# Sums over the values in three rounded fp32r products, and spread over three slots, in a two-layer cross-attention kernel

## Reference

```python
def _cross_attention(q_in, kv_in, wq, bq, wk, bk, wv, bv, wo, bo, bias_k, bias_v):
    qh = (q_in @ wq + bq).reshape(b, q_len, H, K)        # H = 16, K = 128
    kh = (kv_in @ wk + bk).reshape(b, t, H, K)
    vh = (kv_in @ wv + bv).reshape(b, t, H, K)
    kh, vh = (each with one more key, bias_k or bias_v, at the end)
    logits = jnp.einsum('bqhk,bthk->bhqt', qh, kh) / sqrt(K)
    weights = jax.nn.softmax(logits, axis=-1)
    ctx = jnp.einsum('bhqt,bthk->bqhk', weights, vh).reshape(b, q_len, H * K)
    return ctx @ wo + bo

x = x + _cross_attention(layer_norm(x), context, weights 1)
x = x + _cross_attention(layer_norm(x), context, weights 2)
x = x + gelu(layer_norm(x) @ w_fc1 + b_fc1) @ w_fc2 + b_fc2
```

## Time and profile before

| | |
|---|---|
| three timed executions | 1518.45, 1424.64, 1518.13 us; median 1518.13 |
| the profiled execution | 1426.43 us, its span 1424.7 us |
| PE | busy 1366.2 us, 96% of the span, 11607 matmul records |
| DVE, ACT, POOL | busy 902.9 us (63%), 620.4 us (44%), 307.6 us (22%) |

### The profile page before, as it was taken

The page is one execution under the profiler, slowest core; times in us unless marked ns, Lnnn a source line. Parts: engine busy times, 40 slices in busy tenths (PEclk is TensorE's granted clock), DMA queues, the critical chain, the costliest instruction groups (busy, mean ns, idle before and its releaser), DMA issues. The chain is left out here.

```text
span 1424.7 us, 27588 instructions
## 1 busy us (share of the span) xinstructions
PE 1366.2 (96%) x11607; PEld 1219.9 (86%) x11607; DVE 902.9 (63%) x1876; ACT 620.4 (44%) x1022; POOL 307.6 (22%) x290
## 2 busy tenths in 40 slices
PE   5999999999999999999999999998898999997898
PEld 4889998999999898999999999987887877776787
DVE  4866667576666777666666666668534378886322
ACT  4633433434343564334343434346422337775421
POOL 2201011010110112011011010112863023334654
PEclk9999999999999999999999999999999999998999
DMA  5100000001100000000000000000000000002000
GB/s 154 60 31 1 30 11 21 30 1 31 30 2 31 1 31 1 30 31 1 30 1 31 31 2 30 10 22 23 1 1 9 0 2 2 2 3 64 5 30 29
DMA packets 28012, 30.53 MB, mean 21 GB/s; under 512 B 684, under 2 KB 26868, under 8 KB 27892
## 3 DMA queue, kind: packets, MB, share of 16 engines
q1 hardware_dynamic: 27668, 28.72, 6.3%
q10 hardware_dynamic: 226, 0.10, 0.0%
HBM read 26.73 MB, written 2.10 MB: 20 GB/s over the span
## 5 line engine op out<-in xcount | busy, mean ns | idle before, releaser
L334 POOL TENSOR_TENSOR WLO<-W,WHI 128x512 fp32r<-128x512 f32 x64 | 80.7, 1290 | 765.9 <-DVE WHI L728 765.9
L761 DVE STREAM_TRANSPOSE PRT<-PR 32x256 f32<-32x256 f32 x512 | 223.2, 436 | 8.4
L768 DVE TENSOR_TENSOR CLO<-bank,CHI 128x512 fp32r<-128x512 f32 x128 | 88.0, 691 | 145.6 <-ACT CHI L649 145.6
L626 ACT ACTIVATE KT<-bank,PH 128x512 f32<-128x512 f32 x128 | 88.0, 688 | 186.1 <-PE bank L171 186.1
L169 PE MATMUL bank<-WHI,CHI 128*128 128x256 f32 x576 | 167.5, 291 | 0.0
L170 PE MATMUL bank<-WLO,CHI 128*128 128x256 f32 x576 | 161.5, 280 | 0.0
L171 PE MATMUL bank<-WHI,CLO 128*128 128x256 f32 x576 | 161.0, 280 | 0.0
L169 PE MATMUL bank<-WHI,SRC_HI 128*128 128x256 f32 x504 | 146.2, 290 | 0.0
L170 PE MATMUL bank<-WLO,SRC_HI 128*128 128x256 f32 x504 | 140.9, 280 | 0.0
L171 PE MATMUL bank<-WHI,SRC_LO 128*128 128x256 f32 x504 | 140.8, 279 | 0.0
L791 DVE TENSOR_TENSOR X<-X,bank 128x512 f32<-128x512 f32 x128 | 88.0, 688 | 68.0 <-PE bank L171 67.4
(11 more groups left out here) (230 smaller groups left out, 3124.2 us busy)
## 6 DMA issues: line engine op xcount, KB each, us to landing
W<-in_wall SPq DMA_DIRECT2D x17, 1024.0 KB, 5.6
W<-in_ctx SPq DMA_DIRECT2D x4, 512.0 KB, 6.8
X<-in_x SPq DMA_DIRECT2D x4, 512.0 KB, 8.6
mlp_w<-in_w SPq DMA_DIRECT2D x2, 1024.0 KB, 9.1
out<-X SPq DMA_DIRECT2D x4, 512.0 KB, 2.9
W<-in_wall SPq DMA_DIRECT2D x1, 512.0 KB, 6.5
W<-in_wall SPq DMA_DIRECT2D x2, 256.0 KB, 8.3
W<-in_qw SPq DMA_DIRECT2D x1, 256.0 KB, 2.8
```

The costliest lines, as they stand in the source:

```text
L334: i = e.tensor_tensor(WLO[a][:, j, :, :], W[a][:, j, :, :], WHI[a][:, j, :, :].bitcast(F32), ALU.subtract)
L626: e.activation(KT[:, h, :, 0:S], PROJ[2 + h][:, :].rearrange("p (q k) -> p q k", k=S), ACT.Identity, bias=PH[:, 1, 2 * pair + h:2 * pair + ...
L761: i = e.transpose(PRT[b * S + z:b * S + z + 32, :, b * S + y:b * S + y + 32], PR[b * S + y:b * S + y + 32, :, z:z + 32])
L768: e.tensor_tensor(CLO[:, h, :], bank[3 + h][:, :], CHI[:, h, :].bitcast(F32), ALU.subtract).then_inc(c_lo, 1)
```

## The change

The values are now kept as a rounded part `VH` (written by ACT in `values_out`) and a remainder `VLW` (written by DVE in `values_rest`). The transposed softmax weights `PRT` get a rounded part `PHI` (ACT, `probs_hi`) and a remainder `PLO` (POOL, `probs_lo`). `weighted` makes 24 fp32r matmuls of 128 columns through `three()` in place of eight in fp32. PE's order in a slot is now keys, output(n - 2), queries, values 0, values 1, scores(n), weighted(n - 1): a weighted sum follows its scores by one slot and its output by two. The other engines' orders follow, and so does the head of the feed-forward block.

```diff
+            VH = [sb(f"VH{a}", [P, GT, 256], F32R, scope=ph) for a in range(2)]
+            VLW = [sb(f"VLW{a}", [P, GT, 256], F32R, scope=ph) for a in range(2)]
...
@@ gpsimd
+                    def probs_lo(u):
+                        for h in range(2):
+                            e.wait_ge(p_hi, 2 * u + h + 1)
+                            part = slice(h * GT, (h + 1) * GT)
+                            e.tensor_tensor(PLO[:, part, :], PRT[:, part, :], PHI[:, part, :].bitcast(F32),
+                                            ALU.subtract).then_inc(p_lo, 1)
...
+                        before = apply_at(n - 1)
+                        if before is not None:
+                            norm_lo(e, norm, *before)
...
+                        if n:
+                            probs_lo(n - 1)
+                        if g == 2 and pair + 1 < NL * HP + 1:
                             split(pair + 1, 1 - a)
@@ tensor
                     def weighted(u):
-                        e.wait_ge(v_out, 2 * u + 2)
-                        e.wait_ge(pt_out, u + 1)
+                        e.wait_ge(v_lo, 2 * u + 2)
+                        e.wait_ge(p_lo, 2 * u + 2)
                         if u:
                             e.wait_ge(x_settled, 2 * u)
                         for h in range(2):
                             for p in range(GT):
-                                i = e.matmul(bank[3 + h][:, p * P:(p + 1) * P],
-                                             V[u % 2][:, p, h * K:(h + 1) * K],
-                                             PRT[:, h * GT + p, :], start=True, stop=True)
+                                ks = slice(h * K, (h + 1) * K)
+                                i = three(e, bank[3 + h][:, p * P:(p + 1) * P], VH[u % 2][:, p, ks],
+                                          VLW[u % 2][:, p, ks], PHI[:, h * GT + p, :], PLO[:, h * GT + p, :],
+                                          True, True)
                             i.then_inc(c_done, 1)
...
                         keys(n)
...
+                        if n == 2:
+
+                            weighted(0)
+                        elif n > 2:
+                            output(n - 2)
...
                         queries(n)
                         values(n, 0)
...
-                        weighted(n - 1)
                         values(n, 1)
...
                         scores(n)
-                        output(n - 1)
+                        if n > 1:
+                            weighted(n - 1)
...
-                    for q in range(4):
-                        up(q)
+                    up(0)
+                    up(1)
+                    output(SLOTS - 2)
+                    up(2)
+                    up(3)
                     e.wait_ge(sub_done, SLOTS)
                     bias_turns(NL - 1, G - 1, (TB[1], None), SLOTS - 1)
                     weighted(SLOTS - 1)
+                    up(4)
                     e.wait_ge(ptb_out, NL * G)
                     norm_turn(e, norm, NL, 1, TB)
+                    up(5)
                     output(SLOTS - 1)
-                    e.wait_ge(fc2_lo, 1)
+                    up(6)
+                    up(7)
                     e.wait_ge(norm.scaled, (NL * G + 2) * DC)
                     norm_turn(e, norm, NL, 2, TB)
@@ scalar
+                    def probs_hi(u):
+                        e.wait_ge(pt_out, u + 1)
+                        for h in range(2):
+                            part = slice(h * GT, (h + 1) * GT)
+                            e.activation(PHI[:, part, :], PRT[:, part, :], ACT.Copy).then_inc(p_hi, 1)
...
                     for n in range(1, SLOTS):
...
+                        if n > 2:
+                            weighted_out(n - 2)
+                        exponential(n - 1)
...
                         keys_out(n)
...
+                        probs_hi(n - 1)
                         queries_out(n)
                         values_out(n, 0)
...
-                        weighted_out(n - 1)
                         values_out(n, 1)
...
-                        exponential(n)
@@ vector
+                    def values_rest(n, j):
+                        e.wait_ge(v_out, 2 * n + j + 1)
+                        e.tensor_tensor(VLW[n % 2][:, 2 * j:2 * j + 2, :],
+                                        (PROJ[2 + j] if n else PROJ[j])[:, :].rearrange("p (t n) -> p t n", n=256),
+                                        VH[n % 2][:, 2 * j:2 * j + 2, :].bitcast(F32), ALU.subtract).then_inc(v_lo, 1)
...
+                        if n >= 2:
+                            weighted_rest(n - 2)
...
                         softmax(n - 1)
...
+                        if n >= 2:
+                            settle(n - 2)
...
-                        weighted_rest(n - 1)
                         if g == 2 and pair + 1 < NL * HP + 1:
                             round_set(pair + 1, 1 - a)
...
+                        values_rest(n, 0)
+                        values_rest(n, 1)
                         shifted(n)
-                        settle(n - 1)
```

More of the change, by code:

```diff
@@ L345, in _ @@
                                     ALU.subtract).then_inc(w_split, 1)
[L346 to L348 removed]
+                    def probs_lo(u):
[4 more added lines that the diff above has]
+                                            ALU.subtract).then_inc(p_lo, 1)
+                    for n in range(SLOTS):
+                        pair, a, g = unit(n)
+                        before = apply_at(n - 1)
+                        if before is not None:
+                            norm_lo(e, norm, *before)
+                        if apply_at(n) == (NL, 0):
+                            norm_lo(e, norm, NL, 0)
+                        if n:
+                            probs_lo(n - 1)
+                        if g == 2 and pair + 1 < NL * HP + 1:
                             split(pair + 1, 1 - a)
[L350 to L351 removed]
+                    probs_lo(SLOTS - 1)
                     e.wait_ge(fc2_hi, 1)
@@ L363, in _ @@
                         if q == 1:
+                            norm_lo(e, norm, NL, 1)
+                        if q == 3:
+                            norm_lo(e, norm, NL, 2)
                             e.wait_ge(fc2_hi, 2)
@@ L540, in _ @@
                         if bias is not None:
-                            e.wait_ge(q_out, 2 * n + 2)
-                            bias_turns(*bias, PROJ, n - 1)
-                        weighted(n - 1)
[L544 to L550, removed]
+                            if last_turn:
+                                e.wait_ge(norm.scaled, (NL * G + 1) * DC)
+                            else:
+                                e.wait_ge(sub_done, n)
+                            bias_turns(*bias, (TB[1], TB[0]), n - 1)
+                        if n == 2:
+                            output(0)
+                        values(n, 1)
+                        if turned_now is not None and not last_turn:
+                            e.wait_ge(q_out, 2 * n + 2)
                             norm_turn(e, norm, *turned_now, PROJ)
+                        if bias is not None:
+                            L, bg = bias
+                            e.wait_ge(ptb_out, L * G + bg + 1)
+                            e.wait_ge(bw_out, L + 1)
                         if g == 0:
@@ L665, in _ @@
                     queries_out(0)
-                    for c in range(DC):
-                        scale_chunk(e, 0, 1, c, PROJ)
-                    exponential(0)
                     ctx_round(2)
@@ L671, in _ @@
                     for n in range(1, SLOTS):
-                        bias, took, now = bias_at(n), stats_at(n), apply_at(n)
+                        bias, took, before = bias_of(n - 1), stats_at(n), apply_at(n - 1)
+                        if n > 2:
+                            weighted_out(n - 2)
+                        exponential(n - 1)
+                        if before is not None:
+                            for c in range(DC):
+                                scale_chunk(e, *before, c, PROJ)
                         keys_out(n)
@@ L675, in _ @@
                             ctx_round(3)
+                        if n == 2:
+                            weighted_out(0)
+                        if apply_at(n) == (NL, 0):
+                            for c in range(DC):
+                                scale_chunk(e, NL, 0, c, TB)
+                        probs_hi(n - 1)
                         queries_out(n)
@@ L678, in _ @@
                         if bias is not None:
-                            bias_out(*bias, PROJ[0])
-                        weighted_out(n - 1)
+                            bias_out(*bias, TB[1])
                         values_out(n, 1)
-                        if now is not None and now[0] == NL:
-                            for c in range(DC):
-                                scale_chunk(e, *now, c, PROJ)
-                        elif now is not None:
```

(4 more changed lines are left out.)

117 lines of the change are left out of this document (68 added, 49 removed).

## The result

| kernel | median of 4, us | lowest, highest |
| --- | --- | --- |
| before | 1472.61 | 1424.64, 1518.45 |
| after | 1525.63 | 1480.38, 1570.94 |

The ratio is 1.0383 with a 95% interval of 1.0339 to 1.0428: slower, as forecast. Each kernel's four executions are two pairs some 90 us apart (before 1424.6 and 1427.1, then 1518.1 and 1518.5; after 1480.4 and 1480.6, then 1570.6 and 1570.9), and the ratio compares the shorter pairs. The execution of after that was profiled is a longer one, 1570.64 us; those 90 us lie in one stretch behind the slots, so the slots can be read against those of before as they are.

A forecast was written before the change was run, and what follows sets the result against it. The prediction took PE, busy 96% of the span, as the bound. Products +57.3, layer-norm slots +4 and feed-forward head -7 gave +54 us on 1426.4, 1480.8, ratio 1.038; scaled to the median, 1576, range 1465 to 1610.

The forecast's parts named there:

- the load is the floor: Weighted sums on PE: loading 128 stationary columns sets each fp32r product's pace, 0.1115 us; this case has 65%.
- Rival 1: Weighted sums: columns, not the load, set the price, 58 ns or less a product; kernel faster, 1399 us, ratio 0.981; 7%.
- rival 2: Weighted sums: loads partly overlap, a product between 0.074 and 0.1 us; 1434 us, 1526 on the median; 9%.
- rival 3: Weighted sums: short fp32r matmuls fall to fp32's rate, 0.213 us a product; 1636 us, ratio 1.147; 12%.
- The products: Weighted sums on PE: 24 fp32r products, 2.68 us, replace 1.78; +0.90 us a slot, +57.3 us over 64.
- The other engines: Slots: added work on DVE (88 us), POOL (168) and ACT (some 77) never reaches PE; costed at nothing.
- rival 4: Slots: the longer chain over ACT, DVE and POOL starves PE; 1 us each slot gives +64, 1545 us; 7%.
- The slots with the layer norm: About ten slots where DVE's cover is thin: 0.5 us each allowed, +4 us, bounds 0 and 15.
- The head of the feed-forward block: At its start most of PE's 5.7 us wait for POOL goes: -7 us, bounds -12 and +2.
- The sum: Whole kernel: 57.3 + 4 - 7 = +54 us on the profiled 1426.4, giving 1480.8, ratio 1.038.
- The median: Whole kernel: ratio applied to the median, 1518.1 x 1.038 = 1576 us; 1481 if it falls among shorter executions.

The follow-up runs named there:

- experiments 3 and 4: Changed kernel, all slots but the first: 3 with 64 moving columns in weighted sums, 1494.71 to 1495.39 us; 4 with 64 stationary columns, 1405.73, 1407.07, 1496.24, 1496.29.
- experiment 2: Changed kernel with two fp32r products in place of three in each weighted sum, third operand still made: 1425.59, 1426.15, 1516.72 and 1517.1 us.
- experiment 1: Changed kernel with plain fp32 weighted sums, remainders still made and waited for: 1424.59 to 1428.24 us in seven executions, 1516.92 to 1519.35 in three.
- experiment 5: Changed kernel's order with plain fp32 sums, no rounded parts or remainders: 1514.17 to 1517.23 us in six executions, ratio 1.0618 to before.
- experiment 9: Changed kernel's order with fp32 sums, plus ten extra fp32r matmuls ahead of the small-attention loop: median 1424.14 us, ratio 0.9968 to before.

## Why the prediction was right

**The step that decides: the load is the floor.** Forecast 0.1115 us a product, measured 0.111, with half the moving columns 0.111, with half the stationary columns 0.059. Rival 1 (columns) and rival 2 (loads that overlap) fall with experiments 3 and 4, rival 3 (fp32's rate of 0.213) with the slot of 15.18. That an fp32r load keeps the pace of an fp32 one was inferred from durations alone (188 and 193 ns before, 192 after); experiment 2 shows it, 16 records of either kind in a slot of 14.29. The figure of 107 ns from the Trainium skill, "TensorE: Matmul & The Clock Gate", LDWEIGHTS, is 4% under what the products show; its rule that the price goes with the loaded columns agrees with 0.111 and 0.059. The gap of about 81 ns in the same page's Back-to-back issue gap is not what any run here shows for fp32r with 128 loaded columns. (Rival 2 called 0.081 the middle of 0.074 to 0.1; the middle is 0.087, which would have made it +20 us for the slots and not +10.)

**The products.** Forecast +0.90 us a slot and +57.3 in all; measured +0.89 against fp32 sums in the same order (15.18 - 14.29), +0.87 against before, and 54.4 in all. The difference lies in the first slots. The second and third distances between scores are 18.90 and 15.25 us in experiment 1 and 18.91 and 15.30 with three products, so there, where PE waits anyway, the 0.89 costs nothing. (The first distance has no weighted sum in it. It varies by itself, 17.49 us in experiment 1 and 16.06 after, with the clock: the grant is at 0.50 there for 6.8 and for 3.4 us.)

**The other engines.** DVE +90 us (forecast 88), POOL +178 (168), ACT +59 (77). The new rounding on ACT is 74.1 by its group, as forecast; with the order alone ACT is busy 8 us less than before (612.4 by that page), and the rest of the difference was not followed up. In the ordinary slots none reaches PE, and the chain leaves the 2.4 us to spare that were worked out. "None reaches PE, so I cost them at nothing" fails in the second slot, by what rival 4 named. The steps of the layer norm on DVE take 0.41 us each alone and 1.35 to 1.39 beside a subtraction on POOL, and `probs_lo` now puts one there. The second slot of after, and below it the same step in experiment 5:

```profile
62.42 3.31 DVE L129 TENSOR_SCALAR XN<-X,mv,rs 128x256 f32<-128x256 f32 x4
62.92 2.66 POOL L355 TENSOR_TENSOR wl<-PRT,wh 128x512 fp32r<-128x512 f32 x2 [7.55 <-ACT wh L690]
65.88 1.06 PE L138 MATMUL pair<-ident,XN 128*128 128x128 f32 x8 [1.71 <-DVE XN L129]
```

```profile
63.87 1.38 DVE L129 TENSOR_SCALAR XN<-X,mv,rs 128x256 f32<-128x256 f32 x4
```

Four steps take 3.31 us in place of 1.38, and PE waits 1.71 for them. Rival 4 needed such a delay in every slot; the trace has it in the few slots with a layer norm.

**The slots with the layer norm.** Forecast +4, measured near +1: over the seven slots around the middle norm the distances between scores grow by 6.2 us where seven ordinary ones grow by 6.0, and in the last two slots by 0.9 beyond that. The norm's cover held: around the middle norm the four steps of L129 are slowed beside POOL in the same way (two of them take 2.68 us), but PE doesn't wait for them there.

**The first slots.** The sum gave them the 0.90 of every slot. The first distance between scores is 17.12 us before and 16.06 after, the second 15.15 and 18.91, the third 15.56 and 15.30: together +2.4, close to three times 0.87, but by other means. In the second slot some 1.8 us come with the order and 1.9 with the side work (16.99 in experiment 5, 18.90 in experiment 1), and 1.7 of these 1.9 are the wait for the slowed layer norm just shown. No step of the forecast had this.

**The head of the feed-forward block.** Forecast -7. From the last scores to the loop's first matmul were 1159.5 - 973.2 = 186.3 us and are 1212.5 - 1028.6 = 183.9, though one weighted sum (2.7) more stands in this stretch and the last one is 0.9 dearer: -2.4 - 3.6 = -6.0. Part of it is the clock, which the forecast didn't have: before, the grant falls at 995.1 for 6.8 us, in the wait of 5.7 us, and the matmuls behind it run slower, some 1.6 us by the rows (an estimate: eight transposes take 1.62 us to the next start, and 0.109 us each, 0.87 in all, at the full clock; the four matmuls of 512 columns that follow 1.79 in place of 0.93). After, it doesn't fall there. The head is where the order's own gain comes from; it pays 1 to 2 us of it back in the first three slots (49.9 us in experiment 5, 48.7 in experiment 9, 47.8 before).

**The sum** was +54 on 1426.4, 1480.8; the shorter executions of after are 1480.4 and 1480.6. The terms were off by 1 to 3 us each (products and norm slots too large, the head's gain too, the first slots at 0.9 each), and these errors cancel: the step that carries the change was right, but a match to half a microsecond is luck. By the rows the slots bring 55.2 us (996.7 - 941.5), the head -2.4 and the start 0.2, 53.0 of the 54.1; the rest lies behind it, and was not found.

**The median.** 1576 stood for a median among the longer executions, and 1481 for one among the shorter. The four split evenly, and the median of 1525.6 lies between the pairs, where no execution is. That it lies in the range, near the middle of 1465 to 1610, is chance, and so is its match with the 1526 of rival 2; the ratio of the shorter pairs, 1.0383, is what bears the forecast of 1.038 out. The step that the longer time scales with the kernel, 1518.1 x 1.038 = 1576, was off in size: what makes an execution longer is the clock of one loop that the change doesn't touch, so it adds its 90 us to either kernel, and 1518.1 + 54 = 1572 is nearer to the 1570.8 measured.

## What to carry to other kernels

Before splitting an fp32 matmul into fp32r products, look at what sets its pace: at 128 moving columns or fewer it is the load of the stationary operand, 0.11 us for 128 columns, two fp32 records cost as much as two fp32r products, and three products are simply half as dear again. Read that pace from distances between starts, not from durations, and from the rows with the shortest moving operand that the trace has. Work put on a second engine can also slow the first without any wait between them, as POOL's subtractions did to DVE's layer norm: look for the same instruction at two durations. And when executions of one kernel fall into two groups, find the stretch in which they differ before scaling anything by a median.

## What was not expected of the hardware

The small-attention loop runs at either level of PE's clock with PE busy 99% of it: 124 us for 1855 matmuls at a granted clock of 1.00, 214 us for 1867 at 0.50, and once it has fallen behind the wait of 2.73 us it can stay down to the loop's end. In the same kernel it goes either way from one execution to the next (nine of twenty of before at 1518 on one chip, 18 of 54 on all). With ten dense matmuls ahead of the loop, or sixteen in its early steps, none of the 42 executions that had one or the other or both stayed down, where the same three kernels without them did in 9 of 20, in 6 of 6 and in 6 of 8. What the chip measures to decide this is not settled here.

In the run with 64 moving columns the grant fell inside slots in which PE was busy all the time, and the kernel with less to compute was 14 us slower than the one with more. A busy PE in the profile is thus no sign that its clock is safe.
